# A seven-stage model kernel: the window-attention loop staged over three images, and the retention row sums moved ahead of mixing

## The reference, cut to what matters

```python
x = x + retention(group_norm(x))            # 8 images, 1024 pixels, 128 channels, 8 heads
x = x + conv3x3_int8(group_norm(x))
t = tokens(x)
t = t + windowed_gate(layer_norm(t))
t = t + top2_of_16_experts(layer_norm(t))
t = t + shifted_window_attention(layer_norm(t))     # windows of 32 tokens, 4 heads of 32
t = t + experts4(layer_norm(t), gates from a graph attention over 524288 edges)

def shifted_window_attention(x):            # per image
    x = roll(x, -16)
    q, k, v = split(x @ w_qkv.T + b_qkv)
    sim = q @ k.T / sqrt(32) + rel_pos;  sim[masked] = -inf
    out = softmax(sim) @ v @ w_out.T + b_out
    return roll(out, 16)
```

## Time and profile before

| | us |
|---|---|
| median of 3 runs | 4123.59 |
| lowest, highest | 4115.06, 4146.0 |
| the profiled execution, its own time | 4139.36 |
| its span, first to last instruction | 4137.5 |
| busy in the span: PE, DVE, ACT, POOL | 3008.8, 2744.9, 1716.6, 1532.4 |
| mean granted clock of PE | 0.828 |

### The profile page before, as it was taken

How to read it: one execution, slowest core, us unless ns; L and a number is a source line. 1 busy time by engine, 2 the same in 40 slices (tenths; PEclk the granted TensorE clock), 3 DMA queues, 4 the chain that set the end, 5 groups by cost and what they waited for, 6 DMA issues and landing times.

```text
span 4137.5 us, 50394 instructions
## 1 busy us (share of the span) xinstructions
PE 3008.8 (73%) x13840; PEld 1465.2 (35%) x13840; DVE 2744.9 (66%) x3978; ACT 1716.6 (41%) x3342; POOL 1532.4 (37%) x1280
## 2 busy tenths in 40 slices
PE   0798898988984663887016667766279999999728
PEld 0222222222221321776014444444135555555312
DVE  2677877877873777999965555555156666666557
ACT  0587877777883552554003443333012222221000
POOL 0211211111100345776032111110758888888810
PEclk9999999999996675999556666666689999999868
DMA  6543254144401112787001000011001111111015
GB/s 226 148 123 84 86 133 127 42 117 132 108 36 52 66 71 73 252 260 245 0 22 31 26 26 26 26 36 33 5 21 38 30 31 32 29 27 17 4 52 193
DMA packets 247329, 319.16 MB, mean 77 GB/s; under 512 B 52300, under 2 KB 183436, under 8 KB 246680
## 3 DMA queue, kind: packets, MB, share of 16 engines
q1 hardware_dynamic: 217496, 296.77, 23.3%
q0 software_dynamic: 29696, 20.97, 3.1%
HBM read 170.95 MB, written 146.67 MB: 77 GB/s over the span
## 4 chain that ended last, share of the span: by engine, by line
POOL 19%; issue 16%; PE 14%; DVE 10%; DMA 3%; SPq 3%; another core or an unknown queue 2%; ACT 2%; DVEq 0%; POOLq 0%; ACTq 0%
POOL arena L903 17%; PE banks L1263 2%; PE banks L1325 2%; PE banks L1276 1%; SPq L675 1%; DVE arena L2040 1%; DMA slot_out_dram<-arena 1%; DVE arena L2317 1%; DVE mx L2319 1%; DVE arena L2269 1%; PE banks L1296 1%; POOL sorted_dram L858 1%; DVE arena L2326 1%; PE banks L1335 1%
## 5 line engine op out<-in xcount | busy, mean ns | idle before, releaser
L1385 PE MATMUL banks<-arena 128*128 128x512 f32 (+1 forms) x1920 | 746.1, 530 | 105.5 <-DVE arena L2418 87.9
L2418 DVE TENSOR_TENSOR arena<-arena 128x1280 f32<-128x1280 f32 x320 | 472.0, 1491 | 353.4 <-PE banks L1385 262.2
L1385 PEld LDWEIGHTS banks<-arena 128*128 128x128 f32 x1920 | 369.9, 193 | 550.6 <-issue 453.8
L903 POOL DMA_INDIRECT arena<-dst_dram,edges_now x336 | 408.4, 1216 | 102.4 <-issue 102.4
L903 POOL DMA_INDIRECT arena<-src_dram,edges_now x336 | 407.0, 1211 | 99.5 <-issue 97.9
L1976 DVE TENSOR_TENSOR keys<-banks,arena 128x512 f32<-128x512 f32 x512 | 317.8, 683 | 114.9 <-PE banks L956 74.9
L2223 DVE TENSOR_TENSOR keys<-keys 128x1024 f32<-128x1024 f32 x264 | 376.8, 1488 | 2.3
L1976 DVE TENSOR_TENSOR arena<-banks,arena 128x512 f32<-128x512 f32 x512 | 318.1, 683 | 88.7 <-PE banks L956 67.4
L1557 ACT ACTIVATE arena<-arena 128x512 f32<-128x512 f32 x512 | 285.7, 618 | 149.9 <-PE banks L979 80.0
L956 PE MATMUL banks<-arena 96*128 96x512 bf16 x1024 | 288.7, 395 | 50.7 <-DVE arena L1976 41.4
L1557 ACT ACTIVATE keys<-keys 128x512 f32<-128x512 f32 x512 | 279.3, 616 | 89.6 <-PE banks L979 88.4
(11 more groups left out here) (389 smaller groups left out, 5794.0 us busy)
## 6 DMA issues: line engine op xcount, KB each, us to landing
sorted_dram<-zeros SPq DMA_DIRECT2D x8, 8192.0 KB, 27.3
arena<-in_w SPq DMA_DIRECT2D x150, 384.0 KB, 4.4
arena<-parts_dram SPq DMA_DIRECT2D x192, 128.0 KB, 4.9
experts_dram<-keys SPq DMA_DIRECT2D x64, 256.0 KB
keys<-experts_dram SPq DMA_DIRECT2D x8, 2048.0 KB, 8.5
parts_dram<-nodes SPq DMA_DIRECT2D x16, 768.0 KB, 3.3
slot_out_dram<-arena SPq DMA_DIRECT2D x40, 256.0 KB, 4.4
arena<-sorted_dram SPq DMA_DIRECT2D x150, 64.0 KB, 3.8
```

What stands on the lines that cost most here:

```text
L903: pool.indirect_dma_start(to[:, s, t, :], None, table[:, :], bass.IndirectOffsetOnAxis(edges_now[:, s, n, t:t + 1].bitcast(U32), 0)).then_ ...
L1385: last = pe.matmul(banks[:, bank, 0:part.shape[1]], ohl[:, s, t, :], part, start=False, stop=False, skip_group_check=True)
L2418: dve.tensor_tensor(rh[:, t % RH], oha[:, s, t:t + 1, :].broadcast_to([P, VALS, NB]), vals[:, s, t, :].unsqueeze(2).broadcast_to([P, VALS, ...
```

## The change

The third loop now works on three images in each turn: one leaves (projection back, second norm, features), one attends, one enters (expert rows, first norm, projections). It takes ten turns; the first and last two have only some of the parts. The block index k orders all parts. On every engine the steps of the leaving and the entering image stand at fixed blocks. The banks are dealt out anew: similarity 0, leaving image 1 and 3, transposes 2, values' product 4, counts 5 (all nine chunks into one sum), entering image 6 and 7. `similarity` now reads a q that lies in four 128-row tiles, one for each head, zero outside the head's 32 rows (POOL fills the zeros once, ACT writes the strips), against all 128 rows of k, and is issued one block ahead. The entering image has its own tiles (two `x_entered`, `xc_entered`, `sq_entered`). The weighing and the sum of the expert rows move from DVE to POOL, behind the gathers, and POOL gathers image 0 before it waits for the sort's end. SP loads images further ahead and stores them in the later turn. In the retention loop PE runs `norm(r-1)` ahead of `beside` and `mix(r)`.

```diff
...
+        COUNT_AT = ((), (), (0, 1), (2, 3), (), (4,), (5, 6), (7, 8))
...
+            def gather_made(m):
+                weight = pair_weight[:, bass.ds(m, 1), :].rearrange("p a j -> p (a j)")
+                pool.tensor_copy(rows_now, pair_row[:, bass.ds(m, 1), :].rearrange("p a j -> p (a j)"))\
                     .then_inc(rows_copied, 1)
-                pool.wait_ge(rows_copied, b + (IMAGES + 1))
-                pool.wait_ge(ln_src, b * 2 + (IMAGES - 1))
-                take_wait(place_step, 0, b * 2 + 2 * IMAGES)
+                pool.wait_ge(rows_copied, m + (IMAGES + 1))
+                since(pool, made_turned, m * 2)
+                take_wait(place_step, 0, m * 2 + 2 * IMAGES)
                 for j in range(PAIRS):
                     pool.indirect_dma_start(made[:, j, :], None, slot_out_dram[:, :], bass.IndirectOffsetOnAxis(
                         rows_now[:, j:j + 1].bitcast(U32), 0)).then_inc(made_in, 16)
-                pool.wait_ge(made_in, b * (16 * PAIRS) + 16 * PAIRS)
-                take_wait(place_step, 0, b * 2 + (2 * IMAGES + 1))
+                pool.wait_ge(made_in, m * (16 * PAIRS) + 16 * PAIRS)
+                take_wait(place_step, 0, m * 2 + (2 * IMAGES + 1))
+                pool.wait_ge(place_step, m * 2 + (2 * IMAGES + 3))
+                pool.tensor_tensor(made, made, weight.unsqueeze(2).broadcast_to([P, PAIRS, C]), ALU.mult).then_inc(made_summed, 1)
+                pool.wait_ge(made_summed, m * 2 + 1)
+                pool.tensor_tensor(made[:, 0:BLOCKS], made[:, 0:BLOCKS], made[:, BLOCKS:PAIRS], ALU.add)\
+                    .then_inc(made_summed, 1)
+            pool.wait_ge(x2_in, 16 * IMAGES + 16)
+            pool.wait_ge(pairs_placed, IMAGES + 1)
+            pool.memset(arena[:, 4 * L:8 * L], 0.0).then_inc(zero_ready, 1)
+            gather_made(0)
+            pool.wait_ge(cnt_step, 1)
+            pool.partition_all_reduce(counts_max[:], counts[:], P, bass.bass_isa.ReduceOp.max).then_inc(cnt_step, 1)
+            with pool.Fori(0, IMAGES - 1) as turn:
+                gather_made(turn + 1)
...
-                    beside(b, r, attend, head, tail, fresh)
-                    if attend:
-                        mix(b, r)
                     if attend and r:
                         norm(b, r - 1)
                     if tail and r == 0:
                         norm(b - 1, ROUNDS - 1)
+                    beside(b, r, attend, head, tail, fresh)
+                    if attend:
+                        mix(b, r)
...
+            def project_window(m, s):
+                pe.wait_ge(rolled, m * 2 + 2)
+                for h in range(HALVES):
+                    if s:
+                        pe.wait_ge(wqk_ready, m * 4 + (h + 1))
+                    pe.matmul(banks[:, 6 + h, :], wqkv[:, s * P:(s + 1) * P], L2["xr"][:, halves(h)],
+                              start=True, stop=True).then_inc(wqk_mm, 1)
+            def project_values(m):
+                for h in range(HALVES):
+                    pe.wait_ge(wqk_ready, m * 4 + (h + 3))
                     for k in range(4):
                         blk = 4 * h + k
-                        last = pe.matmul(banks[:, h, k * P:(k + 1) * P], L2["xr"][:, blk * P:(blk + 1) * P],
+                        last = pe.matmul(banks[:, 6 + h, k * P:(k + 1) * P], L2["xr"][:, blk * P:(blk + 1) * P],
                                          wqkv[:, 2 * P:3 * P], start=True, stop=True)
                     last.then_inc(wv_mm, 1)
-                pe.wait_ge(wqk_ready, b * 4 + 4)
-                pe.wait_ge(wv_ready, b * 2 + 2)
-
-                def similarity(k):
-                    for j in range(WHEADS):
-                        r = slice(WDIM * j, WDIM * (j + 1))
-                        last = pe.matmul(banks[:, j, (k % 4) * P:(k % 4 + 1) * P], qk2[r, 0, k * P:(k + 1) * P],
-                                         qk2[r, 1, k * P:(k + 1) * P], start=True, stop=True)
-                    last.then_inc(sim_mm, 1)
-
-                for k in range(4):
-                    similarity(k)
+            def similarity(b, k):
+                if k == 0:
+                    pe.wait_ge(wqk_ready, b * 4 + 4)
+                since(pe, sim_biased, b * BLOCKS + k)
+                for j in range(WHEADS):
+                    last = pe.matmul(banks[:, 0, j * P:(j + 1) * P], q_of[:, j, k * P:(k + 1) * P],
+                                     k_all[:, k * P:(k + 1) * P], start=True, stop=True)
+                last.then_inc(sim_mm, 1)
+            def weigh_values(b, k):
+                if k == 0:
+                    pe.wait_ge(wv_ready, b * 2 + 2)
+                pe.wait_ge(sim_norm, b * BLOCKS + (k + 1))
+                since(pe, pt_ready, b * BLOCKS + k)
+                for j in range(WHEADS):
+                    last = pe.transpose(banks[:, 2, j * P:(j + 1) * P], sc[:, k % 2, j, :], ident[:])
+                last.then_inc(pt_turned, 1)
+                if k % 4 == 0:
+                    since(pe, pv_copied, b * 2 + k // 4)
+                pe.wait_ge(pt_ready, b * BLOCKS + (k + 1))
+                for j in range(WHEADS):
+                    r = slice(WDIM * j, WDIM * (j + 1))
+                    last = pe.matmul(banks[r, 4, (k % 4) * P:(k % 4 + 1) * P], v2[:, k, r],
+                                     pt[:, k % 2, j, :], start=True, stop=True)
+                last.then_inc(pv_mm, 1)
...
+            def window_turn(b, s, leave, attend, enter):
+                for k in range(BLOCKS):
+                    if k == 0:
+                        if leave:
+                            project_back(b - 1)
+                        if enter:
+                            turn_made(b + 1)
+                    if k == 1:
+                        if leave:
+                            mean_leave(b - 1)
+                        if enter:
+                            mean_enter(b + 1, 1 - s)
+                    if k == 3:
+                        if leave:
+                            var_leave(b - 1)
+                        if enter:
+                            var_enter(b + 1)
+                    if k == 5 and leave:
+                        features(b - 1)
+                    if attend and k + 1 < BLOCKS:
+                        similarity(b, k + 1)
+                    if enter and k >= 6:
+                        project_window(b + 1, k - 6)
+                    if attend:
+                        weigh_values(b, k)
+                        for n in COUNT_AT[k]:
+                            count_next(b, n)
+                if enter:
+                    project_values(b + 1)
+                    similarity(b + 1, 0)
...
+            def take_window(m, s):
+                for h in range(HALVES):
+                    act.wait_ge(wqk_mm, m * 4 + (2 * s + h + 1))
+                    if s:
+                        last = act.activation(k_all[:, halves(h)], banks[:, 6 + h, :], ACT.Identity, bias=bqk[:, 1:2])
+                    else:
+                        for j in range(WHEADS):
+                            r = slice(WDIM * j, WDIM * (j + 1))
+                            last = act.activation(q_of[r, j, halves(h)], banks[r, 6 + h, :], ACT.Identity, bias=bqk[r, 0:1])
+                    last.then_inc(wqk_ready, 1)
+            def copy_p(b, k):
+                act.wait_ge(pt_turned, b * BLOCKS + (k + 1))
+                since(act, pv_mm, b * BLOCKS + (k - 1))
+                act.activation(pt[:, k % 2].rearrange("p h n -> p (h n)"), banks[:, 2, :], ACT.Copy).then_inc(pt_ready, 1)
+            def copy_x(b, h):
+                act.wait_ge(pv_mm, b * BLOCKS + 4 * (h + 1))
+                since(act, wout_mm, b * 2)
+                act.activation(xs[:, h, :], banks[:, 4, :], ACT.Copy).then_inc(pv_copied, 1)
...
+            def window_turn(b, leave, attend, enter):
                 for k in range(BLOCKS):
-                    act.wait_ge(sim_biased, b * BLOCKS + (k + 1))
-                    for j in range(WHEADS):
-                        last = act.activation(sc[:, k % 2, j, :], sc[:, k % 2, j, :], ACT.Exp, bias=mx[:, k % 2, 1, j:j + 1],
-                                              accum_out=mx[:, k % 2, 2, j:j + 1])
-                        last.then_inc(sim_exp, 1)
-                    if k >= 1:
-                        copy_p(k - 1)
-                copy_p(BLOCKS - 1)
-                for h in range(HALVES):
-                    act.wait_ge(pv_mm, b * BLOCKS + 4 * (h + 1))
-                    act.activation(xs[:, h, :], banks[:, 6 + h, :], ACT.Copy).then_inc(pv_copied, 1)
-                layer_norm(b, 3)
+                    if attend:
+                        act.wait_ge(sim_biased, b * BLOCKS + (k + 1))
+                        for j in range(WHEADS):
+                            act.activation(sc[:, k % 2, j, :], sc[:, k % 2, j, :], ACT.Exp, bias=mx[:, k % 2, 1, j:j + 1],
+                                           accum_out=mx[:, k % 2, 2, j:j + 1]).then_inc(sim_exp, 1)
+                        if k:
```

(92 more changed lines are left out.)

269 lines of the change are left out of this document (105 added, 164 removed).

## The result

The changed kernel took 4183.3 us (median of four executions; the kernel before, beside it, 4121.8). The ratio on record is 1.0119 (95% interval 1.0081 to 1.0157), or 49 us more; the quotient of the two medians, 1.0149, lies inside that interval. The forecast was 4125 us and no difference above 1%. The interval has 1% inside it, so whether the kernel is slower by more than that stays open, but it is clearly slower, and the forecast of +1 us was not met. The ratio on the median that I started from gives 4173 us, inside the range of 4050 to 4180; the median itself is 3 us above it.

What follows compares the result with a forecast made beforehand. No engine was full: a dependent chain passing from engine to engine bound the third loop, and the clock mattered as much. Ends +39 and front -24 gave +15, retention loop -14: +1, so 4125 us on the median; range 4050 to 4180.

Steps and rivals of the forecast that it cites:

- rival (b): Third loop: gaps in every softmax block keep the clock at 0.50, 98.5 us a turn, so 4168 us; chance 0.20.
- step 6: Third loop: expert sum on GpSimd, 7.7 us, slows VectorE by 30%, partly off the chain: 0.5 us a turn.
- Steps 1 to 5: Third loop's turn: similarity, softmax block, side work in series, added waits and clock together give 92.5 us.
- rival (a): Third loop: the clock, once at 1.00, holds through the blocks; 84 us a turn, so 4064 us; chance 0.25.
- ring block: Third loop: one softmax block's chain from similarity through transposes to value matmuls, 6.6 us at clock 0.50, 5.3 at 1.00.
- Step 8: Third loop's ends: ten turns for eight, 741 us from the first similarity instead of 702, so +39.
- Step 7: Third loop's front: image 0's gathers run before the sort ends; first add 27 us earlier, first similarity's end 24 earlier.
- Step 9: Retention loop: row sums moved ahead save 2 us a turn, 7 turns, so -14; bounds -35 and +14.
- the four terms: Retention turn: sums fit the seam 0.6, wait for roots gone 1.4, VectorE's sums earlier 0.9, less 0.9 where ScalarE is late.

Runs made afterwards that it cites:

- e12: Changed kernel with the expert sum back on VectorE and at most two gathers under way: ratio 1.0042, full turns 92.0 to 92.5 us, the third 95.2.
- e11: Kernel before with row sums ahead, image 0's gathers issued before the wait for the sort, at most two gathers under way: ratio 0.9806, turns 88.6 to 89.9 us.
- e3: Changed kernel with GpSimd's product and sum cut to one of 16 and one of 8 blocks, all gathers kept: ratio 1.0008.
- e2: Changed kernel with the expert product and sum back on VectorE, the gathers left on GpSimd: ratio 1.0060.
- e6: Changed kernel with similarity(k+1) ahead of block k's side work, expert sum on VectorE, and turns 1 to 6 of TensorE, ScalarE, VectorE written out: ratio 1.0013.
- e5: Changed kernel with similarity(k+1) ahead of block k's side work and the expert sum on VectorE, turns still looped: ratio 1.0023.
- e4: Changed kernel with similarity(k+1) put ahead of block k's side work and the counts of block k-1 on TensorE: ratio 1.0022.
- e7: Changed kernel with only turns 1 to 6 of TensorE, ScalarE and VectorE written out instead of looped: ratio 1.0096.

## Why the range held and the forecast did not

Measured by the ratio, the time lies inside the stated range, but not for a reason of mine: the range reached so far up for rival (b), a clock that stays low, and that did not happen. The +48 us came from GpSimd's arithmetic, which step 6 priced at a sixth, and from gathers that had no term at all. That the two together stayed inside the range is luck.

**Steps 1 to 5, the turn: right.** Forecast 92.5 us with PE near 70; without GpSimd's two costs 92.0 to 92.5 (last full turn; e12) with PE at 67. Similarity took 1.98 to 2.08 us (2.0 forecast); PE stood 2.51 to 2.54 ahead of the transposes (2.5). One ring block without side work, from value matmuls to value matmuls at 0.50, took 7.0 us (2755.6 to 2762.6 above; 6.6 forecast). The clock was 0.64 to 0.68; rival (a) did not come. The half microsecond between forecast and measurement hides errors that offset: 0.4 us too little for a ring block and 3 us too much for PE's work.

**Step 6, GpSimd: this failed.** I took the mean of the sort's steps, 1607 against 1221 ns, for a slowdown of 30% and charged 0.5 us a turn. The measured price is 3.4 us a turn, six times, and 5.0 us in the sort: 25 us. The mean hid two kinds of step, which the line of min/median/max shows at once: 1210 ns alone, and 1632 and more while GpSimd multiplied for the slots. The rule that I had named and set aside, an exclusive lock of the shared port pair that blocks the loser fully (the Trainium skill, "SBUF — State Buffer", on the shared port pair), is what the runs show. Its condition that GpSimd's instruction reads SBUF as well: the 3.5 us zero fill beside the sort, which reads none, left all five sort steps around it at 1.22 us. Only my price for it, all 7.7 us of GpSimd's time on the chain, was too high: the instructions took 5.95 us and 3.4 of it reached the chain.

**A term was missing: the gathers.** I took their 20 to 25 us to lie beside other work and gave them no price. Even the old loop had paid 3.3 us a turn for them (e11). In the changed loop they are queued during blocks 0 to 2, and DVE and ScalarE were held until about when they had landed: 3.7 us in each turn that gathers, and 6.7 and 2.4 more in the third and fifth: 31 us in all, if turn 0 pays as a full turn does. The hold ends with the landing whatever came before it: the transposes of the third block began 28.97 us into the plain turn in e3 and 28.95 in e2, by different ways, and 25.46 in the turn without gathers. No rival of mine had it. Rival (b) came near in size (98.5 a turn forecast, 99.4 the mean), but by another mechanism, a clock stuck at 0.50; the fast stretches were there, so (b) was not right.

**Step 8, the ends.** Turn 0 took 91.4 us, the 84 forecast and one turn's 7.1 of GpSimd; the last attending turn 79.2 (80); the leaving one 17.2 (22). From 741 forecast to 784.4: 20.4 for the sums, 22.2 for the gathers and 9.1 in the third and fifth turns make 51.7; the six full turns without them were 3.0 less than forecast and the two ends 5.6 less, turn 0 0.3 more: 43.4.

**Step 7, the front: right.** Forecast -27 and -24; measured -27.2 and -25.8.

**Step 9, the row sums: right in kind, too small.** Forecast 2 us a turn, measured 3.6, or 21.4 instead of 14 in all. PE's idle time fell by 8.7 us a turn (16.2 to 7.4), more than the four terms, and its busy time rose by 5.1, since neighbouring groups overlap less in the new order: from the start of one to the start of the next, a mixing group took 0.88 us and now 1.00, a group of scores 0.88 and 0.97, a pair of f32 matmuls 0.96 and 1.06. I had priced neither. The 138.7 us that I named for the old turn was also wrong: it is 143.4.

**Together:** -21.4 + 2 + 5.0 - 25.8 + 83.4 = 43, and 4 behind the loop, is the 47 us.

## What to carry to other kernels

Moving an operation from DVE to GpSimd need not relieve DVE. Here a DVE product of two SBUF inputs and a negate of four numbers a row waited until GpSimd's whole instruction had ended, while a maximum and an addition that reads a bank did not. So ask where in DVE's chain the other's longest instruction will fall, and on which kind of instruction. Don't judge contention from a mean; look at min/median/max of the line, or at a single instance of each. And when a turn is rearranged, look at what GpSimd has queued at each place: 16 gathers at once held another engine for up to 9.5 us in a full turn, and pacing them by twos, on an engine with time to spare, shortened the old loop's turn by 3.3 us with nothing else changed. Where nothing hides the gathers, pacing costs: image 1's took 36 us instead of 22.

## What the hardware showed that I had not expected

- A queue of gathers holds other engines. DVE stood, with its input ready, 1.1 us in the changed kernel's plain turns, 6.1 and 3.9 in its third and fifth, and 7.8 to 9.5 in three turns of e6, until about when all 16 gathers (0.95 us each to issue, 20 us together) had landed; in one turn each of e5 and e6 it went on 9 and 5 us before that. ScalarE's copy came 1.3 us late in plain turns and 8 in e4. With two under way at most no wait called "remote" is left in the full turns. That the engines were waiting for instructions is my guess, from the third turn's jump (e7) and the engine-less "remote"; the trace shows instruction packets in these windows but none that ends with the hold, so the mechanism stays open.
- DVE beside an addition or multiplication of GpSimd: 0.17 became 1.50 us, 0.69 became 2.83, 1.22 became 4.63; beside GpSimd's fill, no change (1.22). DVE's maximum and its addition from a bank kept their 0.69 beside GpSimd's product. GpSimd waits as well: its product took 4.60 us beside the sort and 3.61 elsewhere, and ten of image 0's 16 gathers took 1.9 to 2.0 us each to issue beside the sort instead of 0.95.
